# Another way for the row maxima, later preparation of one layer's weights and new issue orders in a six-layer decoder kernel

## The reference, cut to what matters

```python
x = LN(x + attn_taylor(x))        # a: rope, 16 heads of 16, weights t/sum(t), t = 1 + s + s*s/2
x = LN(x + cross_attn(x, ctx))    # b: projections, softmax
x = LN(x + moe(x))                # c: 8 experts 256->512->256, top 2
x = LN(x + delta_net(x))          # d: convolutions, delta rule, FIR filters, gates
x = LN(x + cross_attn(x, ctx))    # e: no projections, softmax
x = LN(x + fp4_mlp(x))            # f: weights and activations rounded to blocks of 16
```

## Time and profile before

| | |
|---|---|
| median of 3 runs | 3857.47 us (3849.73 to 3866.94) |
| the profiled execution | 3852.97 us, its span 3851.2 us |
| PE busy | 3140.6 us, 82% of the span |
| DVE busy | 2442.1 us, 63% |
| ACT busy | 1448.4 us, 38% |
| POOL busy | 353.0 us, 9% |
| mean granted clock of PE | 0.918 of full |

### The profile page before, as it was taken

The page is one execution under the profiler, slowest core; times in us unless marked ns, Lnnn a source line. Parts: engine busy times, 40 slices in busy tenths (PEclk is TensorE's granted clock), DMA queues, the critical chain, the costliest instruction groups (busy, mean ns, idle before and its releaser), DMA issues.

```text
span 3851.2 us, 52451 instructions
## 1 busy us (share of the span) xinstructions
PE 3140.6 (82%) x19460; PEld 2356.0 (61%) x19460; DVE 2442.1 (63%) x5735; ACT 1448.4 (38%) x2874; POOL 353.0 (9%) x710
## 2 busy tenths in 40 slices
PE   1577888989898988889898988989898988977554
PEld 0355666757575766757575766757575766756342
DVE  5224656676766757677666757676766766675743
ACT  1323343444434343443434343443434343432211
POOL 1000101010010101010010101010010101010100
PEclk9688989999999999999899989999999999998666
DMA  2232343332342333432332333422342333322010
GB/s 74 47 90 72 86 85 78 83 75 64 83 91 61 78 85 78 93 76 53 88 85 61 82 81 78 95 63 64 81 93 61 78 86 78 79 60 53 15 24 3
DMA packets 591192, 275.33 MB, mean 71 GB/s; under 512 B 464712, under 2 KB 553440, under 8 KB 590944
## 3 DMA queue, kind: packets, MB, share of 16 engines
q1 hardware_dynamic: 488544, 137.75, 19.0%
q10 hardware_dynamic: 102400, 134.23, 11.4%
HBM read 156.55 MB, written 14.68 MB: 44 GB/s over the span
## 4 chain that ended last, share of the span: by engine, by line
PE 56%; DVE 19%; ACT 11%; issue 6%; DMA 3%; SPq 3%; POOL 2%; PEldq 0%; DVEq 0%; PEld 0%; POOLq 0%; ACTq 0%
PE bank L709 20%; PE bank L930 7%; ACT pt_f L1191 5%; PE bank L786 5%; PE bank L766 3%; DVE nm_f L1574 2%; PE bank L753 2%; SPq L531 2%; DMA kT_f<-split_f 2%; PE bank L1091 2%; ACT split_f L1202 2%; PE bank L1012 2%; PE bank L718 2%; PE bank L1032 1%; PE bank L1023 1%
## 5 line engine op out<-in xcount | busy, mean ns | idle before, releaser
L930 PE MATMUL bank<-c_w,c_hb 128*128 128x256 f32 x2048 | 511.8, 392 | 6.6 <-PEq L1164 4.5
L709 PE MATMUL bank<-xTc,c_w 128*128 128x256 f32 x2048 | 501.1, 393 | 9.4 <-DVE yc L1718 6.6
L1191 ACT ACTIVATE pt_f<-bank 128x512 f32<-128x512 f32 x768 | 416.7, 595 | 238.7 <-PE bank L766 237.1
L1574 DVE TENSOR_REDUCE nm_f<-bank 128x2 f32<-128x512 f32 x512 | 315.4, 682 | 244.0 <-PE bank L753 240.9
L709 PEld LDWEIGHTS bank<-xTc,c_w 128*128 128x128 f32 x2048 | 390.2, 197 | 73.0 <-issue 10.8
L930 PEld LDWEIGHTS bank<-c_w,c_hb 128*128 128x128 f32 x2048 | 379.5, 195 | 71.9 <-issue 14.2
L1293 ACT ACTIVATE c_hb<-bank,cols 128x256 f32<-128x256 f32 x512 | 214.3, 470 | 554.9 <-PE bank L709 554.9
L1794 DVE SCALAR_TENSOR_TENSOR region<-vpad,cols,region 128x256 f32<-128x256 f32 x1024 | 414.5, 478 | 0.0
L766 PE MATMUL bank<-qT_f,kT_f 102*128 102x256 bf16 (+1 forms) x1536 | 285.7, 291 | 146.9 <-ACT pt_f L1191 97.1
L766 PEld LDWEIGHTS bank<-qT_f,kT_f 102*128 102x128 bf16 (+1 forms) x1536 | 109.3, 99 | 329.9 <-ACT pt_f L1191 229.0
L1191 ACT ACTIVATE xTf<-bank 128x512 f32<-128x512 f32 x112 | 66.8, 596 | 403.6 <-PE bank L718 375.3
(11 more groups left out here) (307 smaller groups left out, 5193.7 us busy)
## 6 DMA issues: line engine op xcount, KB each, us to landing
c_w<-in_c_w ACTq DMA_DIRECT2D x256, 512.0 KB, 4.7
gram_scratch<-region SPq DMA_DIRECT2D x32, 256.0 KB, 6.3
x<-in_x SPq DMA_DIRECT2D x16, 256.0 KB, 3.0
x<-in_ctx SPq DMA_DIRECT2D x16, 256.0 KB, 3.1
ctxb<-in_ctx SPq DMA_DIRECT2D x16, 256.0 KB, 3.0
out_dram<-x SPq DMA_DIRECT2D x16, 256.0 KB, 2.2
qT_f<-split_f SPq DMA_TRANSPOSE x192, 3.4
kT_f<-split_f SPq DMA_TRANSPOSE x192, 3.4
```

The lines of the kernel that those rows point to most:

```text
L709: mm = pe.matmul(out_ap, l, r, start=(i == 0), stop=(i == len(pairs) - 1))
L930: mm = pe.matmul(PS[use][:, t * D:(t + 1) * D], c_hb[:, k, t * P:(t + 1) * P], c_w2[:, e % W_SLOTS, k, :], start=(k == 0), stop=(k == HC - 1))
L1191: act.activation(dst, PS[use].rearrange("p (c s) -> p c s", c=c), func, **kw).then_inc(*PS.drained(use))
L1574: dve.tensor_reduce(a.nm[:, :, h], PS[use].rearrange("p (t s) -> p t s", t=T), AX.X, ALU.max, negate=True)\
```

## The change

1. The three parts of the maximum go into a small tile `m3` (128 x 96), which PE turns with 2 transposes into one bank, ACT copies it to `mT` (48 x 256, bf16), and a DMA from SP writes it as rows 99 to 101 of `qT`. PE waits for that DMA before the first score. The 32 transposes and the copies of ACT and DVE are gone.
2. Rounding and turning f's weights becomes a layer w with segments of its own in step 0; the loads other than a's are issued by SP in step 0 behind x and ctx. The angles are made in a_rope of batch 0.
3. `absent()` is gone: the counts of bank uses are computed for the layers that are there.
4. Layer a's constant term is computed once a batch, 8 matmuls with one column into a bank (`a_sv`); ACT copies it and adds it as a bias when it copies the weighed values, now in two instructions of 256 columns instead of one of 512.
5. `BODY` has a new order, and steps 0, 1, 2, 16 and 17 have orders of their own (`EDGE`).

```diff
-e_in e_part1 c_in e_part2 d_in c_gate e_turnq e_turnk d_proj c_comb e_max0 c_up0a e_max1 c_up0b e_max2 e_max3 c_down0a
-e_shift e_again d_conv e_score0 e_score1 e_weigh0 e_score2 d_silu e_weigh1 c_down0b e_score3 e_weigh2 e_weigh3 d_token
...
-d_gated b_max2 c_up7a b_max3 b_shift c_up7b d_logit c_down7a b_again d_weight c_down7b b_score0 d_mix b_score1
-b_weigh0 b_score2 b_weigh1 b_score3 b_weigh2 b_weigh3 d_ms d_out b_out c_res d_res c_apply d_apply b_res b_apply
+w_gu0 w_turn0 w_gu1 w_turn1 w_gu2 e_in w_turn2 e_part1 d_in c_in e_part2 c_gate e_turnq d_proj c_comb e_turnk e_max0
+c_up0a e_max1 c_up0b e_max2 c_down0a w_gu3 e_max3 e_shift c_down0b c_up1a e_again c_up1b c_down1a e_score0 e_score1
+e_weigh0 d_conv e_score2 e_weigh1 d_silu c_down1b e_score3 e_weigh2 w_turn3 e_weigh3 d_token e_out c_up2a c_up2b
...
+b_turnk c_up6b d_scan1 b_max0 d_scan2 b_max1 d_scan3 b_max2 d_turn d_gate d_gated b_max3 b_shift c_down6a c_down6b
+d_logit c_up7a b_again d_weight c_up7b d_mix b_score0 d_ms c_down7a b_score1 b_weigh0 b_score2 b_weigh1 b_score3
+b_weigh2 b_weigh3 d_out b_out d_res c_down7b c_res d_apply c_apply b_res b_apply
+EDGE = {n: order.split() for n, order in (
+    (0, """
...
+f_round1 d_apply c_down0a f_down c_down0b c_up1a f_res f_apply w_gu0 w_turn0 w_gu1 a_score0 a_score1 a_weigh0 a_score2
+a_weigh1 a_score3 a_weigh2 a_weigh3 a_out b_in b_ctx a_res a_apply w_turn1 b_x c_up1b c_down1a c_down1b c_up2a c_up2b
...
+c_up6a c_up6b c_down6a b_proj b_part1 b_part2 b_turnq b_turnk w_gu2 b_max0 w_turn2 b_max1 b_max2 b_max3 b_shift
+b_again b_score0 b_score1 b_weigh0 b_score2 w_gu3 w_turn3 b_weigh1 w_dn0 b_score3 w_dn1 b_weigh2 b_weigh3 c_down6b
+c_up7a b_out c_up7b b_res c_down7a w_turn4 c_down7b w_scale c_res b_apply c_apply
+"""),
...
+            def max_rows(b, l):
+                sp.wait_ge(*PS.taken(f"{l}_rT", b))
+                sp.dma_start(at_.qT[MAX0:MAX0 + 3, :, :], at_.mT).then_inc(*att[l]["max_in"].up)
...
             def turn_again(b, l, a):
+                use = f"{l}_rT"
+                o = PS[use].bitcast(BF16)
                 pe.wait_ge(*att[l]["shift"](b))
-                for i in range(4):
-                    split_turn(b, l, a, SLOT, f"{l}_rT", 0, i)
+                pe.wait_ge(*PS.free(use, b))
+                for t in range(T):
+                    mm = pe.transpose(o[0:3 * H, t * P:(t + 1) * P], a.m3[:, t, :, :].rearrange("p i h -> p (i h)"), identb[:, :])
+                mm.then_inc(*PS.full(use))
...
-                if taylor:
-
-                    for c in range(T):
-                        pe.matmul(o, a.v[:, c, 4 * g:4 * g + 4, :].rearrange("p h v -> p (h v)"), ones[:, 0:S],
-                                  start=(c == 0), stop=False, skip_group_check=True)
+                if taylor and g == 0:
+                    pe.wait_ge(*PS.free("a_sv", b))
+                    for k in range(4):
+                        for c in range(T):
+                            mm = pe.matmul(PS["a_sv"][:, k:k + 1], a.v[:, c, 4 * k:4 * k + 4, :].rearrange("p h v -> p (h v)"),
+                                           ones[:, 0:1], start=(c == 0), stop=(c == T - 1), skip_group_check=True)
+                    mm.then_inc(*PS.full("a_sv"))
...
-            pe.wait_ge(s_seta, 11 + FCH)
-            pe.wait_ge(s_setv, SETUP_V)
             pe.wait_ge(s_const, CONSTANTS)
-            for s, k in ((s_wa, 3), (s_wb, 4), (s_wc, 2), (s_wd, 7)):
-                pe.wait_ge(s, 16 * k)
...
-            def absent(n, l):
-
-                for (segment, k), (at, cnt) in PS.segments.items():
-                    if segment[0] == l:
-                        yield segment
-                        pe.wait_ge(PS.drained_sem[k], n * PS.count[k] + at + 1)
-                        pe.sem_inc(PS.full_sem[k], cnt)
-                        pe.sem_inc(PS.drained_sem[k], cnt)
```

More of the change, by code:

```diff
@@ L98 @@
          + ["c_res", "c_apply"])
+FOUR = [x for i in range(4) for x in (f"w_gu{i}", f"w_turn{i}")] + ["w_dn0", "w_dn1", "w_turn4", "w_scale"]
 BODY = """
[L103 to L105 removed]
@@ L106 @@
[L106 to L110, removed]
@@ new lines @@
+""".split()
+EDGE = {n: order.split() for n, order in (
+    (0, """
+d_in d_proj d_conv d_silu d_token d_norm e_in e_part1 d_chan e_part2 d_gram d_blocks d_grams d_fir0 d_place d_fir1
+d_fir2 d_fir3 d_one4 e_turnq d_fir4 e_turnk e_max0 e_max1 e_max2 e_max3 e_shift e_again e_score0 e_score1 e_weigh0
+e_score2 c_in c_gate d_two4 d_twb4 d_one5 e_weigh1 d_fir5 c_comb d_two5 c_up0a d_twb5 d_one6 d_fir6 d_two6 d_sums
+d_scan0 d_scan1 d_scan2 d_scan3 d_turn d_gate d_gated d_logit d_weight d_mix e_score3 e_weigh2 e_weigh3 c_up0b d_ms
@@ new lines @@
+e_res d_proj a_proj e_apply f_in a_rope w_turn3 c_comb c_up0a c_up0b c_down0a f_up0 d_conv c_down0b d_silu w_dn0
+a_part1 c_up1a f_up1 c_up1b d_token a_part2 a_turnq c_down1a c_down1b c_up2a d_norm c_up2b f_round0 a_turnk f_round1
+f_down f_res f_apply d_chan c_down2a a_score0 c_down2b a_score1 d_gram a_weigh0 d_blocks d_grams a_score2 d_fir0
+d_place c_up3a c_up3b d_fir1 a_weigh1 a_score3 a_weigh2 c_down3a a_weigh3 d_fir2 c_down3b d_fir3 w_dn1 a_out b_in
+c_up4a b_ctx a_res c_up4b a_apply d_one4 d_fir4 c_down4a b_x d_two4 b_proj d_twb4 c_down4b d_one5 d_fir5 d_two5
@@ new lines @@
+e_turnq c_comb w_turn4 w_scale d_conv c_up0a c_up0b c_down0a c_down0b d_silu c_up1a c_up1b e_turnk e_max0 c_down1a
+d_token c_down1b e_max1 c_up2a d_norm c_up2b e_max2 d_chan e_max3 e_shift c_down2a c_down2b e_again d_gram c_up3a
+c_up3b d_blocks d_grams d_fir0 d_place d_fir1 e_score0 c_down3a e_score1 e_weigh0 e_score2 e_weigh1 e_score3 e_weigh2
+e_weigh3 d_fir2 c_down3b e_out a_norm c_up4a c_up4b e_res d_fir3 a_proj e_apply c_down4a c_down4b c_up5a c_up5b
+c_down5a f_in d_one4 a_rope d_fir4 d_two4 f_up0 d_twb4 d_one5 a_part1 d_fir5 d_two5 f_up1 d_twb5 a_part2 d_one6 d_fir6
@@ new lines @@
+"""),
+    (17, """
+w_gu0 w_turn0 w_gu1 w_turn1 w_gu2 w_turn2 w_gu3 w_turn3 w_dn0 c_in e_in e_part1 d_in e_part2 d_proj e_turnq c_gate
+c_comb c_up0a c_up0b d_conv c_down0a e_turnk c_down0b e_max0 d_silu e_max1 d_token e_max2 d_norm e_max3 c_up1a c_up1b
+c_down1a e_shift d_chan d_gram c_down1b e_again d_blocks d_grams d_fir0 d_place e_score0 e_score1 e_weigh0 w_dn1
+e_score2 e_weigh1 e_score3 w_turn4 e_weigh2 d_fir1 d_fir2 d_fir3 e_weigh3 e_out a_norm e_res a_proj e_apply f_in
+d_one4 d_fir4 a_rope d_two4 f_up0 d_twb4 a_part1 d_one5 d_fir5 d_two5 f_up1 a_part2 d_twb5 d_one6 d_fir6 d_two6 d_sums
```

422 lines of the change are left out of this document (256 added, 166 removed).

## The result

The changed kernel takes 3748.45 us (median of 4 runs, 3729.13 to 3753.34) against 3857.11 us for the kernel before on the same chip: a ratio of 0.9707, 95% interval 0.9667 to 0.9748. It is faster, as forecast, but by 109 us and not by 241; the time lies outside the range. The profiled execution took 3748.86 us with a span of 3747.1.

What follows compares the result with a forecast made beforehand. PE's work plus short waits was taken to bound full steps, one batch's chain the ends. Start 60, full steps 124 and ends 57 give 241 us off 3857.5: 3616 us, forecast 3575 to 3665 (57%), wider range 3535 to 3705.

Steps and rivals of the forecast that it cites:

- The start: Set-up and step 0: PE begins at about 18.5 us instead of 87.1; 60 us gained, bounds 50 and 66.
- Term 1, the transposes: Full steps: 64 transposes a step become four, gaining 4.0 us of PE work a step.
- Term 2, the waits: Layers e and b, round the transposes: covered waits gain 1.5 us a step; a 6.3 us landing would lose 5.5.
- The sign of being wrong: DMA of the maxima in the middle steps: a landing over 4 us would show the forecast wrong; 1.8 to 3 expected.
- The Trainium skill's rule: DMA of the maxima: it would run on 3 engines, landing near 3 us instead of 1.8, about 0.5 us a step worse.
- Term 3, the constant term: Layer a's attention: single-column matmuls gain 1.5 us a step, with 0.5 and 2.35 as the ends.
- Term 4, the order: Full steps: the new order gains 2.5 us a step, 1.0 of it from the clock; between -2 and +6.
- Terms 1 to 4: Full steps: 9.5 us a step gained, 124 us over 13 steps; ends 3 to 15 us a step.
- The ends: Steps 1, 2, 16, 17 and 18: 12, 12, 12, 20 and 1 us gained, together 57; ends 20 and 80.
- The waits stay: Full steps: ACT's pace and the DMA of the maxima leave 4 us a step gained; 3688 us, 20% chance.

Runs made afterwards that it cites:

- b_cnt: The kernel before with one part of the change, no counting for absent layers at the two ends; 3831.30 us, ratio 0.9935.
- u_bc: u_body with the constant term as before, so the order before with the DMA in place of the transposes; 3710.03 us, ratio 0.9627.
- u_all: The changed kernel with order, constant term and transposes all as before in the full steps; 3708.99 us, ratio 0.9613.
- u_body: The changed kernel with the order before in steps 3 to 15 and 18, edge orders and new operations kept; 3697.44 us, ratio 0.9587.
- u_const: The changed kernel with layer a's constant term as before, matmuls against 256 columns of ones; 3747.69 us, ratio 0.9690.
- h_on: The changed kernel with the order before up to layer b's context and the new order after it; 3707.40 us, ratio 0.9616.
- h_no: The changed kernel with the new order up to layer b's context and the order before after it; 3749.29 us, ratio 0.9737.
- o_a1: u_body with c_down3b, d_fir2 and d_fir3 moved ahead of layer a's scores, leaving one expert segment among them; 3749.23 us, ratio 0.9738.
- o_fill: o_a1 plus eight f32 matmuls of constants at a_weigh0 whose result is overwritten; 3757.61 us, ratio 0.9740.
- o_a3: u_body with cover for the DMA of the maxima (3664 us), then c_up4b moved between a_weigh1 and the last scores, c_down4a into its place; 3728.03 us.
- o_up4b: u_body with cover for the DMA of the maxima (3664 us), then c_up4b alone moved between a_weigh1 and the last scores; 3733.71 us.

## Why the prediction was wrong, point by point

- **The start: right.** 60 us, measured 59 by the windows. PE's first transpose of step 0 starts at 20.62 us; 18.5 was forecast, before 22 was the mark. One reading in it was off: of the 14 us put down to counting, b_cnt shows 10, and PE there waits for DVE until 77.19.
- **Term 1, the transposes: the work right, its value wrong.** 1024 transposes of 68.1 us became 64 of 9.7, so 3.7 us a step and not 4.0. In the order before, the work fetched nothing (u_bc and u_all), where waits for the DMA and a lower clock in layer e took its place.
- **Term 2, the waits: half wrong.** The chain of copy, issue and landing was put at 3.4 us, with 2.3 for the landing, bounded by 1.8 and 6.3. From the transposes to the score it is 3.3 in step 18 and 6.5 in the full step shown; from issue to score it is 2.5 us in layer b and 5.1 here in layer e, where the new order has two loads of 512 KB go out just ahead. PE waits 33.2 us for this DMA in the twelve steps, 2.8 a step. The sign of being wrong that the prediction names, a landing over 4 us in the middle steps, came. I had named those loads and then priced the landing near the lower bound all the same. Both of its values lie within what the bounds allowed. ACT's 0.7 us behind the experts' evacuations I had not counted. The Trainium skill's rule weighed there (DMA: Bandwidth & Descriptors, Why a DMA increments its semaphore by 16 and not by 1) can't be judged from this: the traces show the time, not the number of engines, and the 2.47 us with nothing beside it lie between the 1.8 and the 3 that the two cases were given.
- **Term 3, the constant term: right beside the order before.** 1.5 us a step forecast, 1.9 in u_body against u_bc; beside the new order the time shows nothing of it (u_const). The single column costs 33.4/256 = 130 ns of PE each, where 119 were estimated from four columns.
- **Term 4, the order: the step that failed.** It was to give 2.5 us a step, with -2 as its worst end, and costs 4.2 (220.7 against 216.5). I had reckoned with new waits as the risk. Against the order before there were none on balance. The clock was the risk, 4.5 us a step of busy time (192.1 against 187.6) where I had it give 1.0: I had priced it as a share of the step that would shrink with the waits, and did not ask what the move of an expert segment does to a stretch that is only scores and weighing, paced by ACT. Two long waits went, and a thin stretch of twenty microseconds came, in which the clock is 0.83 on the mean and below 0.90 in eight of the twelve steps.
- **Terms 1 to 4 together.** 9.5 us a step less were forecast, 3.9 more measured: 13.4 x 13 = 174 us of the miss. The range was too narrow by the prediction's own numbers: its lower end of 3 us leaves out the loss of 5.5 that term 2 names for a landing of 6.3. With it the terms' lower ends sum to 4.0 - 5.5 + 0.5 - 2 = -3.0 us a step, where -3.9 was measured.
- **The ends: under-sized at the end, over-sized at the front.** Step 1: 2 for 12; step 2: 5 for 12; step 16: 31 for 12; step 17: 34 for 20; step 18: 24 for 1. The last is the tail of counting, which could have been read off the trace: the last store is issued 25 us before the span's end. For 16 and 17 I took half of the long waits or less; the own orders took away more: PE's idle time falls from 38 to 14 us in step 16 and from 76 to 47 in step 17. In sum the ends gave 38 us more than forecast (59 + 2 + 5 + 31 + 34 + 24 - 117 = 38). 174 - 38 = 136 is, but for rounding, the miss of 137 between 241 and the 104 of the spans.
- **The rivals.** "The waits stay" (3688) had half the mechanism: PE does wait for the DMA, 42.5 us in the run. But its 4 us a step would still have been a gain. No rival had a full step that gets slower through the clock while work is taken out. Taking work from PE pays at the rate of the busy share only if the clock is left alone.

What stays open: why the clock falls in layer a's attention in one step and not in the next of the same program, and whether density is the property that counts. That the order makes the loss, at the clock and ahead of b_ctx, is shown (u_body, h_on, h_no, o_a1). o_fill and u_const raise the clock of that stretch by adding work there; neither makes the kernel faster. o_a3 and o_up4b are confounded by their own waits.

## What to carry to other kernels

In a kernel whose main engine is the bound and whose clock moves between two levels, as here, an order has two prices: the waits it makes and the clock it leaves. Compare PE's busy time for the same instructions, not only the idle time; a stretch where it grows (3.22 us for 1.93 in the weighing shown) shows up in no list of waits. When a short DMA goes onto the chain, look at what is issued in the one or two microseconds ahead of it and at what stands before its producer in the queue, and price it with the loaded row. And look behind the last store: time there is free to take.

## What the runs showed that was not expected

- Clock: over a stretch of 26 us in layer a's attention it was 1.00 in one step (2.4 GHz throughout) and 0.74 in the next (between 1.2 and 2.4), in the same place of the same program. The slower one had no longer waits in that stretch than the faster one, which even stood still 1.86 us for a DMA behind the last weighing.
- The DMA of 24 KB: 2.5 us from the start of its issue to the first use alone, 4.5 to 5.6 with two loads of 512 KB issued in the 1.3 us before it, and 2.5 again with the same loads issued 1.5 us behind it.
- 3.7 us of PE work a step, replaced by a DMA with 3.9 us of exposed waits (46.8/12), gave nothing. Three moved segments that left 1.0 us of these waits gave 23 to 33 us; whether they would have given something beside the old transposes was not run.
- Eight f32 matmuls of filler (some 1.9 us) at the thin place raised the clock there from 0.86 to 0.95 and made a step 1.0 us longer.
